# The two gates of a graph network: who multiplies the last products, in how many pieces the result goes out, and which PSUM banks it passes

## The reference, cut to what matters

```python
def _gate(h, q, Wg, bg, Wq, bq):
    B, L, F = q.shape                     # 8, 64, 768; 32 nodes in each of the 8 groups
    N = h.shape[0] // B
    h3 = h.reshape(B, N, F)
    hg = jnp.einsum('bnf,gf->bng', h3, Wg[:, :F])
    qg = jnp.einsum('blf,gf->blg', q, Wg[:, F:]) + bg
    attn = jax.nn.sigmoid(hg[:, :, None, :] + qg[:, None, :, :])
    qi = jnp.einsum('bnlf,blf->bnf', attn, q)
    alpha = jax.nn.sigmoid(jnp.einsum('bnf,gf->bng', h3, Wq[:, :F]) + jnp.einsum('bnf,gf->bng', qi, Wq[:, F:]) + bq)
    hn = alpha * jnp.tanh(qi) + (1.0 - alpha) * h3
    return hn.reshape(B * N, F)

h = jax.nn.relu(_rgcn(x, W_rel1, ...)); h = _gate(h, ...)
h = jax.nn.relu(_rgcn(h, W_rel2, ...)); h = _gate(h, ...)
```

## Time and profile before

| | |
|---|---|
| median of 3 runs | 1336.73 us |
| the profiled execution's own time | 1335.77 us |
| its span | 1334.0 us |
| TensorE busy | 1286.0 us (96%) |
| VectorE, ScalarE, GpSimd busy | 978.7, 786.3, 215.8 us |
| mean granted TensorE clock | 0.993 |
| first gate, first select to start of `Wq` | 134.34 to 254.12 us |
| second gate, start of `Wq` | 466.75 us |

### The profile page before, as it was taken

One profiled execution on the slowest core, in us unless ns is written; L12 is line 12 of the kernel. 1 busy time (PEld: TensorE's weight loads), 2 busy tenths in 40 slices (PEclk: granted clock), 3 DMA queues, 4 the chain that ended last, 5 costly groups with the idle time before them and its releaser, 6 DMA issues.

```text
span 1334.0 us, 24333 instructions
## 1 busy us (share of the span) xinstructions
PE 1286.0 (96%) x10108; PEld 1119.7 (84%) x10108; DVE 978.7 (73%) x1771; ACT 786.3 (59%) x1298; POOL 215.8 (16%) x108
## 2 busy tenths in 40 slices
PE   9999999999999989999999999999999999999998
PEld 8999644699844479889988999889999999988986
DVE  8775677775677788688878668967677777779555
ACT  3455888645698756566747455645455554447344
POOL 0210587300297600002021001010000000000100
PEclk9999999999999999999999999999999999999899
DMA  9275356145354324152464452444455555233200
GB/s 362 74 251 188 128 180 163 38 141 176 134 188 121 95 96 161 45 210 64 186 238 143 177 183 91 165 157 155 165 178 186 195 190 178 72 129 144 84 1 25
DMA packets 31120, 195.35 MB, mean 146 GB/s; under 512 B 4241, under 2 KB 4369, under 8 KB 15010
## 3 DMA queue, kind: packets, MB, share of 16 engines
q1 hardware_dynamic: 31010, 193.79, 42.9%
HBM read 183.55 MB, written 3.93 MB: 141 GB/s over the span
## 4 chain that ended last, share of the span: by engine, by line
PE 80%; DVE 9%; ACT 6%; POOL 3%; issue 1%; DMA 1%; POOLq 0%; SPq 0%; DVEq 0%; ACTq 0%
PE PS L370 63%; PE PS L1177 6%; PE PS L1186 4%; PE PS L375 3%; PE PS L777 2%; POOL WK L1388 2%; DVE WL L313 1%; POOL WL L320 1%; ACT WH L306 1%; DVE SM L634 1%; ACT PS L1255 1%; PE PS L1534 1%; DMA RT<-AS 1%; PE PS L1522 0%; ACT WK L2100 0%
## 5 line engine op out<-in xcount | busy, mean ns | idle before, releaser
L313 DVE TENSOR_TENSOR WL<-w,WH 128x768 fp32r<-128x768 f32 x366 | 352.6, 974 | 156.6 <-ACT WH L306 154.6
L306 ACT ACTIVATE WH<-w 128x768 fp32r<-128x768 f32 x381 | 315.6, 841 | 242.4 <-PE PS L370 236.3
L370 PE MATMUL PS<-XS,WH 128*128 128x256 f32 x2256 | 407.3, 283 | 2.4 <-DVE XS L584 1.4
L370 PEld LDWEIGHTS PS<-XS,WH 128*128 128x128 f32 x2256 | 347.0, 188 | 7.2 <-issue 2.8
L370 PE MATMUL PS<-XS,WL 128*128 128x256 f32 x1128 | 317.4, 281 | 0.0
L370 PEld LDWEIGHTS PS<-XS,WL 128*128 128x128 f32 x1128 | 212.4, 188 | 0.0
L1313 DVE TENSOR_TENSOR WK<-PS,WK 128x1024 f32<-128x1024 f32 x128 | 151.6, 1220 | 51.5 <-ACT PS L1255 51.5
L1388 POOL TENSOR_TENSOR WK<-WK 128x1024 f32<-128x1024 f32 x64 | 152.9, 2392 | 195.4 <-ACT WK L1252 195.4
L370 PE MATMUL PS<-WH,GS 128*128 128x256 f32 x864 | 160.8, 284 | 4.8 <-issue 1.4
L1255 ACT ACTIVATE PS<-PS 128x1024 f32<-128x1024 f32 x128 | 127.3, 1012 | 25.5 <-PE PS L1177 20.5
L370 PEld LDWEIGHTS PS<-WH,GS 128*128 128x128 f32 x864 | 135.7, 190 | 7.6 <-issue 4.0
(11 more groups left out here) (295 smaller groups left out, 2073.6 us busy)
## 6 DMA issues: line engine op xcount, KB each, us to landing
w<-f2W_in SPq DMA_DIRECT2D x40, 1152.0 KB, 5.5
w<-Wrel_in SPq DMA_DIRECT2D x12, 1152.0 KB, 7.0
WK<-qrep_in SPq DMA_DIRECT2D x16, 768.0 KB, 6.1
w<-f1Wi_in SPq DMA_DIRECT2D x8, 1152.0 KB, 6.4
w<-f1Wo_in SPq DMA_DIRECT2D x8, 1152.0 KB, 5.2
w<-f3Wqkv_in SPq DMA_DIRECT2D x6, 1152.0 KB, 14.8
RT<-qg_rows SPq DMA_DIRECT2D x16, 384.0 KB, 6.5
RT<-AS SPq DMA_DIRECT2D x32, 192.0 KB, 6.8
```

What stands on the lines that cost most here:

```text
L306: A.e.activation(w_hi(i), w_raw(i), ACT.Copy).then_inc(*hi("w", i))
L313: V.e.tensor_tensor(w_lo(i), w_raw(i), w_hi(i), ALU.subtract).then_inc(*lo("w", i))
L370: ins = T.e.matmul(o, l, r, start=i == 0 and first, stop=i == n - 1 and last, skip_group_check=lint)
```

## The change

- **Bank places.** A function `place(p, q)` gives the pair of banks. In odd pairs q = 1 and q = 2 change places.
- **TensorE's order.** Every pair from 2 on selects 0, 2, 1 instead of 0, 1, 2. ScalarE's order stays as it was: 0, 2, 1, and 0, 1, 2 for the last two pairs.
- **The last pair's third product.** For p = 31, q = 1 ScalarE writes the sigmoid back into PSUM, and VectorE makes the product (`weigh_both`), between its other two. GpSimd makes 31 products a gate instead of 32.
- **The result's pieces.** Three pieces: nodes 0 to 191 (groups 0 to 5), 192 to 223 (group 6), 224 to 255 (group 7). The first one's lower part is on GpSimd, the other two on VectorE. The upper parts wait for `q_in` of groups 5, 6 and 7.
- **VectorE's end.** `sum_out(7)` comes straight behind `q_in(6)`, before any lower part.
- **Fillers.** The group between the sums of pairs 30 and 31 goes; 2 behind the sums of pair 31 and 3 behind `turn_q(7)` stay.

```diff
-BRIDGE = {"gate": (2, 2, 3), ...
+BRIDGE = {"gate": (2, 3), ...
+        def place(p, q):
+            return 3 - q if q and p % 2 else q
-        QI = ((0, 224), (224, 256))
+        QI = ((0, 192), (192, 224), (224, 256))
         def prod(n, p, q):
-            return pool if q == 1 else vec, "prod" + n, p, q
+            return pool if q == 1 and p < NPR - 1 else vec, "prod" + n, p, q
...
-                    o = bank_at(2 + 2 * q + i, ("sg" + n, p, q, i),
-                                (act, "sig" + n, p, q) if q == 1 else (vec, "prod" + n, p, q))
+                    o = bank_at(2 + 2 * place(p, q) + i, ("sg" + n, p, q, i),
+                                (act, "sig" + n, p, q) if q == 1 and p < NPR - 1 else (vec, "prod" + n, p, q))
...
             for p in range(2, NPR):
-                for q in range(3):
+                for q in (0, 2, 1):
                     select(p, q)
...
             for p in range(NPR - 2, NPR):
                 sums(p, 0)
                 sums(p, 1)
-                bridge("gate" + n, p - NPR + 2, 0)
+            bridge("gate" + n, 0, 0)
             turn_q(7)
-            bridge("gate" + n, 2, 0)
-            T.wait_ge(vec, "lower", "qi" + n, 1)
+            bridge("gate" + n, 1, 0)
+            T.wait_ge(pool, "lower", "qi" + n, 0)
+            T.wait_ge(vec, "lower", "qi" + n, 2)
...
-                if q == 1:
+                if q == 1 and p < NPR - 1:
                     free_sg(A, n, p)
-                    A.e.activation(SG[p % NSG][:, :, 1024:1536], SP[q].rearrange("p (u n) -> p u n", u=2),
+                    A.e.activation(SG[p % NSG][:, :, 1024:1536], SP[place(p, q)].rearrange("p (u n) -> p u n", u=2),
                                    ACT.Sigmoid).then_inc(*act("sig" + n, p, q))
                 else:
-                    A.e.activation(SP[q], SP[q], ACT.Sigmoid).then_inc(*act("sig" + n, p, q))
+                    A.e.activation(SP[place(p, q)], SP[place(p, q)], ACT.Sigmoid).then_inc(*act("sig" + n, p, q))
...
             for i, (n0, n1) in enumerate(QI):
-                A.wait_ge(vec, "qi" + n, (6, 7)[i])
+                A.wait_ge(vec, "qi" + n, 5 + i)
...
+            def weigh_both(p):
+                V.wait_ge(act, "sig" + n, p, 1)
+                V.e.tensor_tensor(SG[p % NSG][:, :, 1024:1536], SP[place(p, 1)].rearrange("p (u n) -> p u n", u=2),
+                                  GQ[p // 4 % 2][:, 1024:1536].unsqueeze(1).broadcast_to((P, 2, 512)),
+                                  ALU.mult).then_inc(*vec("prod" + n, p, 1))
...
                 weigh(p, 0)
+                if p == NPR - 1:
+                    weigh_both(p)
...
-            for i, (n0, n1) in enumerate(QI):
-                if i:
-                    sum_out(7)
+            sum_out(7)
+            for i, (n0, n1) in tuple(enumerate(QI))[1:]:
+                if i == 2:
                     q_in(7)
                 vec_lower(ASv[:, 1, :, n0:n1], qiT[:, :, n0:n1], ASv[:, 0, :, n0:n1], "qi" + n, i)
...
-            for p in range(NPR):
+            for p in range(NPR - 1):
                 s = SG[p % NSG][:, :, 1024:1536]
...
+            n0, n1 = QI[0]
+            G.wait_ge(act, "upper", "qi" + n, 0)
+            G.e.tensor_tensor(ASv[:, 1, :, n0:n1], qiT[:, :, n0:n1], ASv[:, 0, :, n0:n1],
+                              ALU.subtract).then_inc(*pool("lower", "qi" + n, 0))
```

More of the change, by code:

```diff
@@ L26 @@
 WARM = (5, 8, 8, 8, 8, 6, 5)
-BRIDGE = {"gate": (2, 2, 3), "f0c": (4, 5, 5), "g3": (4,), "f3": (2, 5), "one": (9, 14)}
+BRIDGE = {"gate": (2, 3), "f0c": (4, 5, 5), "g3": (4,), "f3": (2, 5), "one": (9, 14)}
 GADD = 6
@@ L1312, in weigh @@
                 free_sg(V, n, p)
-                V.e.tensor_tensor(SG[p % NSG][:, q // 2, 0:1024], SP[q], GQ[p // 4 % 2][:, 0:1024],
+                V.e.tensor_tensor(SG[p % NSG][:, q // 2, 0:1024], SP[place(p, q)], GQ[p // 4 % 2][:, 0:1024],
                                   ALU.mult).then_inc(*vec("prod" + n, p, q))
+            def weigh_both(p):
[3 more added lines that the diff above has]
+                                  ALU.mult).then_inc(*vec("prod" + n, p, 1))
             feed_vec(gh + 6)
```

## The result

The changed kernel takes 1333.07 us (median of 20 executions, 1330.49 to 1338.2) beside 1337.25 for the kernel before on the same chip: a ratio of 0.9971, with an interval of 0.9963 to 0.998. By this ratio it is 3.9 us less, 2.7 to 4.9; the two medians differ by 4.2. The forecast was 3.5 us and 1333.2 us. Run once more later, the changed kernel gave 0.997 (0.996 to 0.998). The profiled execution has a span of 1328.9 us against 1334.0, so 5.1 us less.

A forecast was written before the change was run, and what follows sets the result against it. Two loops of nearly one length were taken to bound the steady pairs, a chain of waits the gate's end. Gains of 1.87 and 1.67 us by gate, 3.5 in all, took 1336.73 to 1333.2; range 1330.6 to 1336.6.

The forecast's parts named there:

- The steady pairs: Pairs 12 to a gate's end: four pairs fall from 13.06 to 12.93 us, taken as 0.5 us a gate.
- main rival: Steady pairs gain nothing, the third select still holding the sums; only the end is won, 2.1 us, 1334.6; chance 0.30.
- two loops: In a steady pair: TensorE's selects, wait, sums; and select 0, sigmoid 0, product 0, next select 0, 3.16 us.
- The start: A gate's first pairs: 0.2 us from pair 1's wait, first gate only, and 0.1 from ScalarE's earlier sigmoids.
- The last product: Pair 31: VectorE's last product starts at 247.1, 0.1 us later than before, costing what the steady part won.
- The pieces: Gate's end: GpSimd's lower part takes 2.65 us, copy at 249.3 instead of 251.53, `Wq` 2.2 us earlier without the meeting.
- The fillers: Gate's end: one group less costs nothing by itself, as TensorE was idle around it; it matters only to the clock.
- The meeting: Gate's end: VectorE's subtraction of 192 values, held by GpSimd's op, takes 0.8 to 1.0 us instead of 0.36.
- second rival: At the gate's end VectorE and GpSimd do not meet: gain 4.2 us, 1332.5; chance 0.17.
- The clock: Granted clock stays 1.00 at gates' ends; rival: idle time drops it to 1.2 GHz, up to 1340.2 us, chance 0.06.

The follow-up runs named there:

- order_only: The kernel before with only the new bank places and TensorE's order 0, 2, 1, the gate's end left old: 1335.1 us, ratio 0.9988.
- tail_only: The changed kernel with the banks and TensorE's order (0, 1, 2) of the kernel before, the new gate's end kept: 1333.03 us, ratio 0.9974.
- act_order: The changed kernel with ScalarE taking 0, 2, 1 in pair 30 too: 1335.23 us in one execution; pair 30 to `Wq` 12.38 and 12.37 us against 13.11.
- no_fillers: The changed kernel without the two groups of filler matmuls at each gate's end: 1333.93 us, ratio 0.998.

## Why the prediction was right

- **Sum.** Forecast 3.5, the ruler says 4.37, the times 3.9 (2.7 to 4.9). Right in mechanism, each part a little small: the gains were put at 1.87 and 1.67 by gate, the ruler has 2.27 and 2.10. That the median of 1333.07 lies 0.1 from the forecast 1333.2 is luck in part. The forecast counted from 1336.73, while the kernel before took 1337.25 beside the changed one, so a larger gain came off a larger time. `Wq` was put at 252.2 and 463.2 and came at 250.72 and 461.27; 1.13 of each is the late transfer and the start of the gate, chance, and the rest is the larger gain.
- **The steady pairs.** The main rival (they give nothing) is refuted: 12.90 for four pairs, forecast 12.93. From pair 12 to 30 this gave 0.69 where 0.5 was taken. Half of the miss is in the sum, since 0.13 per four makes 0.59 over these 18 pairs; the rest is that 0.16 per four was won. The signs that it named are there: PSUM sigmoids at 1.93, third select still waiting for VectorE. `order_only` shows that order and places bring the gain; by which of the two loops they bring it is argued and was not tested apart.
- **The start.** Taken at 0.3 and 0.1 a gate; 0.38 and 0.22 measured. The 0.36 wait at 140.65 is gone.
- **The last product.** It was put 0.1 later than before in absolute time, so that the end eats what the steady pairs won. Pair 30's first select to the last product: 8.04 in the working (239.06 to 247.1), 8.05 in the trace. With the steady pairs' larger gain and without the 1.13 of chance the last product came 0.19 earlier than before, not 0.1 later. `order_only` isolates the loss by the order, 0.68 after 0.69 won.
- **The pieces.** Last product to `Wq`: 5.15 in the working (247.1 to 252.25), 5.06 measured. GpSimd's part: 2.65 forecast from two lengths at a straight slope, 2.64 measured. Its start was 247.95 - 247.1 = 0.85 behind the last product, measured 0.89.
- **The fillers.** "One group less costs nothing by itself" leaves out what the group did: by the rows at 248.12 to 249.36 it waited for the reduction of group 6 and kept the sums of pair 31 behind it. The working's copy at 249.3, straight behind the last product, holds only because this group goes. So the copy was timed rightly, but this edit is a part of the gain at the end and not a matter of the clock alone.
- **The meeting.** The second rival (none happens) is refuted: 1.08 and 1.07 us. The forecast was 0.8 to 1.0, a little short. But its price was 0.26 a gate and not the 0.35 of the working, because the last reduction could not have begun much before: with the subtraction out of the way it waited for TensorE instead, and began 11.43 behind pair 30's first select (249.23 - 237.80) where the changed kernel had 11.71 (249.32 - 237.61). The Trainium skill (SBUF — State Buffer, "SBUF: two separate sides") says that the loser of the shared ports blocks for the other's whole instruction. The traces agree that it ends only behind the other: the subtraction's length changed with its start (1.08, 0.86, 0.88), while its end stayed 0.21 or 0.22 behind GpSimd's in three kernels, the changed one, `tail_only` and `act_order` (249.40 and 249.19; 251.60 and 251.38; 251.77 and 251.56). This 0.21 is less than the 0.36 that it takes alone, so by the recorded times it is not wholly behind; no run shows whether the record of GpSimd's end or the rule is rough there. The Trainium skill names, in the same section, as VectorE's side of the lock operations with two SBUF inputs and those in a two-port mode; the reduction and the copy from PSUM, which kept their 0.55 and 0.56 beside GpSimd, agree with that.
- **The clock.** 1.00 at both gates' ends, as forecast. `no_fillers` shows that the rival was a real one: without the two groups left, the clock fell at one gate's end of two.

What the prediction did not see is that the order, for which most of its working was done, is worth 0.6 us in all in this kernel (184.52 - 183.94). The end's edits are worth 3.8. It had the number that says so (the last product is no earlier), but did not ask what would bring it forward. The answer was one line, ScalarE's order in pair 30, and is worth 0.7 us a gate.

## What to carry to other kernels

When the steady part of a loop gets faster, look at which order the last turns run in: an order written for the old loop gives the gain back at the end, as 0.69 became 0.01 in the first gate here. The lower part moved to GpSimd held VectorE's subtraction with two SBUF inputs until its own end, and not the reduction and the copy from PSUM, so put PSUM readers beside such an operation and subtractions of that kind behind it. Fillers stand in the order of their engine: look at what they wait for, and at what stands behind them. To compare two versions by single traces, cut them at fixed points and leave out stretches with a transfer on the path: here the sums then repeated within 0.05 us, where whole launches differ by several.

## Not expected of the hardware

- The same transfers of 192 KB each let their select begin at a distance of 3.15 to 5.12 us from the pair before in the first gate, and of 3.15 to 4.24 in the second, over all kernels run here. What makes them late was not tried.
- The same idle time of TensorE (0.68 and 1.75 us) left the granted clock at 1.00 in one gate and brought it to 0.50 in the next of the same launch.
- One profiled execution of eleven reached the first gate 3 us late (137.18, the others 134.10 to 134.69), with the same code up to there.
